# Filling the routed regions with zero rows by bulk copies during the attention, instead of sixteen paddings per region later

## The reference

```python
x = x + tanh(g_xattn[0]) * L0_xattn(layernorm(x), ctx, ctx, ...)
x = x + tanh(g_ffn[0])   * L0_ffn(layernorm(x), ...)
x = x + tanh(g_xattn[1]) * L1_xattn(layernorm(x), ctx, mask, ...)   # 16 heads of 64
x = x + tanh(g_ffn[1])   * L1_ffn(layernorm(x), ...)

def L1_ffn(hidden, ...):            # 4096 tokens, 16 experts, 4 chosen per token
    scores = sigmoid(x @ gate_w.T)
    topk_idx, topk_weight = gate(scores + e_bias)
    inter = silu(x @ gate_proj[e]) * (x @ up_proj[e])
    y = sum_k topk_weight[k] * (inter @ down_proj)[topk_idx[k]]
    return y + shared_expert(x)
```

## Time and profile before

| | us |
|---|---|
| median of three runs | 1568.88 |
| lowest and highest run | 1566.62, 1571.58 |
| the profiled execution, whole | 1582.4 |
| its span, first to last instruction | 1579.9 |
| attention, about | 405 to 1088 |
| second sparse layer, about | 1088 to 1580 |

### The profile page before, as it was taken

How to read it: one execution, slowest core, us unless ns; L and a number is a source line. 1 busy time by engine, 2 the same in 40 slices (tenths; PEclk the granted TensorE clock), 3 DMA queues, 4 the chain that set the end, 5 groups by cost and what they waited for, 6 DMA issues and landing times. The chain is left out here.

```text
span 1579.9 us, 28066 instructions
## 1 busy us (share of the span) xinstructions
PE 1209.1 (77%) x9252; PEld 1095.7 (69%) x9252; DVE 936.1 (59%) x2025; ACT 785.4 (50%) x2201; POOL 530.2 (34%) x658
## 2 busy tenths in 40 slices
PE   3777217998589999999999999975578767668774
PEld 2555116988578888888888888864577756557773
DVE  4887664453366666568666777774556423223666
ACT  3555213554266667666657555554445434335442
POOL 4333243563000001100164005542225555655541
PEclk8566557999799999999999999996779978888987
DMA  3349744553400000000133003333744555545796
GB/s 97 120 135 264 179 102 130 145 147 76 136 7 14 8 1 21 28 8 1 41 119 110 15 1 122 121 101 130 225 144 135 175 165 157 157 125 166 252 289 222
DMA packets 140545, 181.33 MB, mean 115 GB/s; under 512 B 22496, under 2 KB 120960, under 8 KB 139904
## 3 DMA queue, kind: packets, MB, share of 16 engines
q1 hardware_dynamic: 113040, 127.90, 28.2%
q0 software_dynamic: 17792, 43.14, 8.6%
q10 hardware_dynamic: 9584, 8.60, 1.9%
HBM read 111.51 MB, written 72.32 MB: 116 GB/s over the span
## 5 line engine op out<-in xcount | busy, mean ns | idle before, releaser
L1617 ACT ACTIVATE attend_s<-attend_s,attend_less 128x128 f32<-128x128 f32 x512 | 198.4, 391 | 109.1 <-DVE attend_less L1758 102.5
L2283 POOL DMA_INDIRECT answers<-moe_yb,moe_dst x160 | 158.7, 992 | 166.4 <-ACT moe_yb L2373 128.8
L1572 POOL TENSOR_TENSOR router_xn<-rest_acc,router_mv 128x512 f32<-128x512 f32 x12 | 12.5, 1044 | 445.6 <-DVE router_rs L1234 389.5
L81 PE MATMUL moe_psU<-moe_wh,moe_xl 128*128 (+1 forms) x384 | 119.0, 310 | 0.3 <-issue 0.3
L2429 DVE TENSOR_TENSOR moe_it<-moe_it,moe_psU 128x256 f32<-128x256 f32 x96 | 40.2, 419 | 132.9 <-ACT moe_it L2355 98.8
L82 PE MATMUL moe_psU<-moe_wl,moe_xh 128*128 (+1 forms) x384 | 117.7, 307 | 1.1 <-issue 0.8
L83 PE MATMUL moe_psU<-moe_wh,moe_xh 128*128 (+1 forms) x384 | 117.4, 306 | 0.5 <-issue 0.5
L1635 ACT ACTIVATE attend_pt<-attend_psS 128x1024 f32<-128x1024 f32 x64 | 65.5, 1024 | 95.6 <-PE attend_psS L1909 95.5
L1202 POOL DMA_INDIRECT slots<-router_row,router_idx x80 | 82.0, 1025 | 82.0 <-DMA router_row<-normed_rows 63.0
L2582 PE MATMUL moe_psI<-const_ident,moe_it 128*128 128x128 f32 x192 | 42.2, 305 | 85.0 <-DVE moe_il L2425 79.6
L1756 DVE SCALAR_TENSOR_TENSOR attend_s<-attend_psS,held_bias 128x1024 f32<-128x1024 f32 x64 | 77.9, 1217 | 44.2 <-PE attend_psS L1902 44.1
(11 more groups left out here) (376 smaller groups left out, 4238.5 us busy)
## 6 DMA issues: line engine op xcount, KB each, us to landing
moe_xg<-slots SPq DMA_DIRECT2D x160, 129.0 KB
moe_both<-answers SPq DMA_DIRECT2D x28, 512.0 KB
router_row<-normed_rows SPq DMA_DIRECT2D x40, 256.0 KB
layer_raw<-in_wi_dram SPq DMA_DIRECT2D x8, 1024.0 KB, 5.0
layer_raw<-in_wo_dram SPq DMA_DIRECT2D x8, 1024.0 KB, 7.0
moe_raw<-in_gex_dram SPq DMA_DIRECT2D x17, 384.0 KB, 5.0
moe_both<-normed_rows SPq DMA_DIRECT2D x24, 256.0 KB
slots<-fill SPq DMA_DIRECT2D x32, 129.0 KB
```

Source lines behind the costliest of these rows:

```text
L81: pe.matmul(out, wl, mh, start=first, stop=False)
L1617: last = nc.scalar.activation(s[:, g, j, :], s[:, g, j, :], ACT.Exp, bias=less[:, g, j:j + 1], accum_out=sm[:, g, j:j + 1])
L2283: nc.gpsimd.indirect_dma_start(out=R.YT[q], out_offset=bass.IndirectOffsetOnAxis(ap=dst[:, r % NM, s:s + 1], axis=0), in_=yb[:, r % NY, s, ...
```

## The change

Paddings per expert go. In their place SP copies `fill` blocks over the whole of every region, in the attention: at each of steps 0 to 7 two regions of part 0 (25 copies of one block each), at each of steps 8 to 15 two regions of part 1 (9 copies each). The source is one block, read again and again. POOL waits for all of part 0's copies before the first row is sent (half-step 17), and SP waits for all copies at the end of `attend`. The table `tail`, its instruction on VectorE and its waits go. In `moe`, the loads of the rows to be sent are issued one or two pairs earlier, and the last four stores of normalised pairs are issued by ScalarE at j = 1, 3, 5 and 7, instead of by SP.

```diff
+        self.blanked = [m.sem(f"blanked{r}") for r in range(2)]
...
+            def blank(q, e):
+                to = R.XS[q][e * REGION[q]:(e + 1) * REGION[q], :].rearrange("(b p) n -> b (p n)", p=P)
+                tile = R.fill[q][e * P:(e + 1) * P, :].rearrange("p n -> (p n)").unsqueeze(0)
+                sp.dma_start(to, tile.to_broadcast([REGION[q] // P, P * WIDE])).then_inc(R.blanked[q], 16)
...
             def body(n, p, h):
                 if turns(n):
                     load(n + 2, p, h + 1)
+                if n < STEPS // 2:
+                    blank(0, 2 * n)
+                    blank(0, 2 * n + 1)
+                else:
+                    blank(1, 2 * n - E1)
+                    blank(1, 2 * n - E1 + 1)
                 routed(AT[2 * n])
                 routed(AT[2 * n + 1])
...
+            def blanked():
+                sp.wait_ge(R.gw_in, 32)
+                for b in R.blanked:
+                    sp.wait_ge(b, 16 * E1)
...
             normed(1, 0)
+            pool.wait_ge(R.blanked[0], 16 * E1)
             send(0, 0, 1)
...
-            def padded(q, e):
-                if e == 0:
-                    sp.wait_ge(table_up, 2 * q + 1)
-                first = sp.value_load(tail[0:1, q, e:e + 1], min_val=0, max_val=E1 * REGION[q] - P)
-                sp.dma_start(R.XS[q][bass.ds(first, P), :], R.fill[q][e * P:(e + 1) * P, :]).then_inc(pad_in, 16)
...
-                if j in (7, 8):
-                    for h in range(2 * j - 10, 2 * j - 8):
-                        load_row(h)
-                if j in (8, 10, 12, 14):
-                    R.store_normed(sp, LAST, (j - 8) // 2)
-                if 7 <= j < FIRST:
-                    for e in range((j - 7) * 4, min(E1, (j - 6) * 4)):
-                        padded(0, e)
+                for n in range(2):
+                    if 2 * (j - NX) + NR + n < EXPERTS:
+                        weights(2 * (j - NX) + NR + n)
+                    if NS + 2 * (j - NX) + n < FORMER:
+                        load_row(NS + 2 * (j - NX) + n)
...
+                if j - 1 in normed_at:
+                    R.store_normed(act, LAST, normed_at[j - 1])
...
-                v.scalar_tensor_tensor(tail[0:1, q, :], cnt[0:1, :], 1.0, R.ebase[0:1, q, :], ALU.add, ALU.add).then_inc(table_up, 1)
```

More of the change, by code:

```diff
@@ L1552, in body @@
                     load(n + 2, p, h + 1)
+                if n < STEPS // 2:
[4 more added lines that the diff above has]
+                    blank(1, 2 * n - E1 + 1)
                 routed(AT[2 * n])
                 routed(AT[2 * n + 1])
-            over(sp, body, lambda: sp.wait_ge(R.gw_in, 32))
+            def blanked():
+                sp.wait_ge(R.gw_in, 32)
+                for b in R.blanked:
+                    sp.wait_ge(b, 16 * E1)
+            over(sp, body, blanked)
         @block.gpsimd
@@ L2048, in moe @@
         table = sb("table", [1, 2, 2, 64], I32)
-        tail = sb("tail", [1, 2, E1], I32)
         psX, psU, psY = ([ps(f"{n}{k}", [P, 512]) for k in range(2)] for n in ("psX", "psU", "psY"))
@@ L2061, in moe @@
             sem(n) for n in ("w_hi", "w_early", "w_late", "t_done", "x_hi", "x_lo", "u_done", "s_up", "i_up", "i_done", "i_hi", "i_lo", "y_done", "y_up", "d_up", "g_up"))
-        made, r_done, r_free, col_up, table_up, pad_in, marked, c_up, c_step, stored, added = (
-            sem(n) for n in ("made", "r_done", "r_free", "col_up", "table_up", "pad_in", "marked", "c_up", "c_step", "stored", "added"))
+        made, r_done, r_free, col_up, table_up, marked, c_up, c_step, stored, added = (
+            sem(n) for n in ("made", "r_done", "r_free", "col_up", "table_up", "marked", "c_up", "c_step", "stored", "added"))
         block = ctx.enter_context(nc.Block(no_gpsimd_drain=True))
@@ L2181, in ready @@
             def ready(q):
-                sp.wait_ge(table_up, 2 * q + 2)
-                sp.wait_ge(pad_in, 16 * E1 * (q + 1))
+                sp.wait_ge(table_up, q + 1)
                 sent_upto(sp, (FORMER, len(SENDS))[q])
@@ L2224, in _ @@
             for j in range(NX, PAIRS_ALL):
-                for k in (2 * (j - NX) + NR, 2 * (j - NX) + NR + 1):
-                    if k < EXPERTS:
-                        weights(k)
-                if j in (7, 8):
-                    for h in range(2 * j - 10, 2 * j - 8):
-                        load_row(h)
-                if j in (8, 10, 12, 14):
-                    R.store_normed(sp, LAST, (j - 8) // 2)
-                if 7 <= j < FIRST:
-                    for e in range((j - 7) * 4, min(E1, (j - 6) * 4)):
-                        padded(0, e)
+                for n in range(2):
[3 more added lines that the diff above has]
+                        load_row(NS + 2 * (j - NX) + n)
                 if j == STARTS_OF[0]:
@@ L2240, in _ @@
                     load_row(FORMER + i // 2)
-                e = j - placed_at - NX - 4
-                if 0 <= e < E1:
-                    padded(1, e)
                 if j == STARTS_OF[1]:
@@ L2477, in tables @@
                 v.tensor_copy(table[0:1, q], psR[0:1, 0:2 * P].rearrange("p (a j) -> p a j", a=2)[:, :, 0:64]).then_inc(table_up, 1)
-                dve.wait_ge(table_up, 2 * q + 2)
+                dve.wait_ge(table_up, q + 1)
                 dve.sem_inc(r_free, 1)
@@ L2605, in _ @@
                 if j + 1 in STARTS_OF:
-                    pe.wait_ge(table_up, 2 * KIND[j + 1] + 2)
+                    pe.wait_ge(table_up, KIND[j + 1] + 1)
                 if j + 1 < PAIRS_ALL:
```

## The result

The changed kernel takes 1610.94 us (median of 4 runs, 1609.13 to 1615.28), the kernel before, run again beside it, 1567.91 us (4 runs, 1566.62 to 1571.58). The ratio is 1.0275, with a 95% interval of 1.0247 to 1.0302: 43 us slower. The forecast was 1869 us, also slower, but by 300 us. The sign and the places of the stalls came as foretold; the size did not. That 1610.9 lies inside the stated range (1610 to 2090) is luck: it lies 1 us from its foot, and the likeliest case had 1740 to 1955. (The paddings that went are one per region, sixteen per part, and not sixteen per region as the title has it.)

The account below looks back on a forecast made before the run. TensorE was taken to bound the attention, memory and SyncE's order the second sparse layer's first stage. 1582.4 profiled, plus 315 for copies, minus 15 gained, gives 1882; less 13.5, 1869 us, range 1610 to 2090.

Parts of the forecast that it names:

- the likeliest case: Attention's copies on five engines near 16.5 GB/s each (14.7 to 20), 1740 to 1955 us; chance 0.38.
- The equal deal: Attention's copies: the outer count is dealt in equal shares, so 25 blocks go to 5 engines and 9 to 9.
- a rival with sixteen engines: Attention: all engines share each copy, 12.5 us per copy, nothing on TensorE waits, 1554 us; chance 0.19, 0.16 with a gain.
- I take 16.5: Rate of one engine copying memory to memory in the attention, in GB/s; gives 40.0 us per copy of part 0.
- the best end: Attention's copies at the fastest rate taken, 23.9 GB/s per engine: 27.6 us per copy, +101 us, 1655 us.
- The rival of five engines at that rate: Attention's copies on five engines at 23.9 GB/s each: +101, 1655 us; chance of five engines, faster, 0.20.
- The estimate of 13.4 GB/s: Attention's copies: the skill's 214 GB/s shared by 16 engines; would add some 474 us in place of 315.
- The sum: Attention: contexts and stores land late behind copies in SyncE's queue, delaying TensorE's turns by 315 us in all.
- +11: Attention, after the first send: two more meetings of a store with copies in SyncE's queue add 11 us.
- The gain: Second sparse layer's first stage: paddings' issue, their bytes and waits for stores removed, 15 us, bounds 0 and 30.
- The stage of 12 shared pairs: Second sparse layer's first stage: a sign that it would take about 55 us instead of 70.
- Share near 5/16: Attention's steps of 470 to 800 us: a sign of a DMA share about 0.3, with 83 GB/s.

Follow-up runs that it names:

- act_stores: Changed kernel with the attention's twelve stores of pairs issued by ScalarE in its own queue, copies still on five engines from SyncE: 1603.88 us, ratio 1.02 to the kernel before.
- spread16: Changed kernel with the same bytes copied, each copy cut to an outer count of 16 with runs of 8,256 bytes: 1553.79 us, ratio 0.9849 to the kernel before.
- spread4: Changed kernel with each copy cut to an outer count of 4, runs of 33,024 bytes: 1754.87 us, ratio 1.1189 to the kernel before.
- before_copies: Kernel before with the region copies and their two waits added in the attention; its paddings and second sparse layer stay: 1648.7 us, ratio 1.0462 to the kernel before.
- act_queue: Changed kernel with the region copies issued by ScalarE in its own queue, still 25 and 9 blocks: 1645.4 us, ratio 1.0437 to the kernel before.
- act_stores_short: Changed kernel with the attention's stores on ScalarE and each copy made as eight transfers of 16,512-byte runs, still five engines: 1610.18 us, ratio 1.0269 to the kernel before.

## Why the prediction was wrong in size and right in kind

**How many engines: right.** The equal deal was taken against a rival with sixteen engines. The share of 0.33 shows five, outer counts of 16, 8 and 4 give 0.66, 0.52 and 0.28, and of a store's 256 records 80, sixteen for each of five engines, are the late ones (act_stores). The rule of the Trainium skill's page "DMA: Bandwidth & Descriptors", section "Why a DMA increments its semaphore by 16 and not by 1", says the same for 25, and the trace agrees. The rival's time, 1554, is also what the same copies cost when they are cut for sixteen engines, 1553.8; but the kernel before took 1576.6 beside that run, so the rival's gain of 15 us was 24, and the match to the microsecond is luck.

**The rate of an engine: the step that failed.** The prediction said "I take 16.5, as the new transfers have large packets", from queue 8's 1.25 MB in 0.3%, and so 40.0 us per copy. It is 27.06 GB/s and 24.4 us. The rounding of 0.3% was not the fault: in the DMA records of the kernel before, queue 8's packets of 16,384 bytes take 1002 ns in the median, 16.4 GB/s. But that is queue 8, instruction, another kind of transfer, and its size says nothing of a copy. The nearest kin of the copies stood in the same trace: the paddings, also from `fill` to `slots`, are 512 runs of 8,256 bytes, and the fastest takes 309 ns, 26.7 GB/s (474 ns in the median, among the other transfers of a busy stage). The windows had 23.9 GB/s per busy engine. The bounds were too low as well: the best end was 27.6 us per copy. The rival of five engines at that rate (+101, 1655 us) was the right mechanism and came nearest in size, and stood at a chance of 0.20. The estimate of 13.4 GB/s from the Trainium skill's 214 GB/s (same page, section "Latency and other measured facts"), shared by sixteen, is not borne out either: the trace has 27 GB/s for each of five engines, and 280 GB/s for sixteen while spread16's copies ran.

**The sum, done again with 24.4 us.** By the same steps: the context turned at 548.2 lands at 427 + 4 x 24.4 + 3 = 528, not late; that of 625.0 at 625, just in time (5.4 late in the trace). The first store lands at 427 + 244 + 3 = 674, the second pair is turned at 677, 32 late (38); the next store lands at 674 + 48.8 = 723, the third pair is turned at 726, 62 late (70). Steps 6's and 7's copies, issued at 735 and 740, need 98 us and end by 834 (831 in the trace), before POOL needs them at 848, so the "+11" and the wait before the first send fall away. That is 62 us instead of 315, and 1582.4 + 62 - 15 - 13.5 = 1616 for the measured 1610.9. That it comes so near is luck in part, as too little lateness (62 for 68) and too little gain (15 for 24 to 29) cancel. The second and third turn come 6 to 8 us later than in this working; the other transfers among the copies, which the working left at nothing, are of this order (16 us over twelve copies).

**The lateness is no constant times the length.** From 24.4 to 30.5 us per copy it goes from 68 to 184 (spread4), since each turn that comes late lets another store meet other copies. The forecast's copy was 64% too long (40.0 against 24.4 us), and its sum 4.6 times the measured one (315 against 68).

**The gain: 15 us taken, 24 to 29 measured.** spread16 gives 24, before_copies against the changed kernel 29. The profiles give more, 491.7 to 450.8 us for the layer, and before_copies has 492.0 in a run within 3 us of its median; how much of these 41 us is the 13.5 of the one profile, the rows do not decide. The stage of 12 shared pairs was to take 55 us and takes 51.4. The prediction valued the earlier row loads at nothing beyond the 15, and they are worth perhaps 6.

**Only one queue.** The working explains the stalls by SyncE's queue. That is what happens, but it is not needed: with the copies in ScalarE's queue the stalls are as long (act_queue).

**The signs foretold.** Share near 5/16: yes. 83 GB/s: 139. Waits of over 50 us on L1239's turn: two of 31.5 and 29.9, and POOL's of 64.5 behind them. TensorE waiting for context from the third step on: once, 3.9 us. A gap of POOL before the first send: none beyond 6.9 us for a row load. No padding, and a shorter first stage: yes. The clock, for which nothing was added, was 0.57 of 2.4 GHz in the window of 650 to 690, in which TensorE was idle 31 of 40 us, and 0.50 from 710 to 730, its level of 1.2, when it had nothing to do at all; from 740 to 780 it was 1.00 again. It cost little: from the third pair's turn to the fourth's it took 22.9 us instead of 21.3.

So the 43 us are some 68 lost in the attention, by copies that use five engines, and 24 to 29 won in the second layer. The two sizes agree with the difference and with the experiments that have one without the other. The version that keeps the gain and not the loss is the one with an outer count of 16 or 8: 1553.8 and 1543.4 us, 0.985 and 0.984 of the kernel before, which their intervals do not tell apart. That is 4% below the changed kernel.

## What to carry to other kernels

Cut a large copy so that its outer count is 16, or 8, and read the DMA share of a step afterwards: a share that stands at 5/16 while the copy runs says that eleven engines are idle. Before large transfers are put into an idle stretch, add up their time on the engines that they will really use, and compare it with the stretch up to the first thing that waits for them all; another queue does not help against full engines, and there a small transfer pays one run of the copy for each of its own records on such an engine. For the price of a transfer that no row shows, look for its nearest kin in the trace, by source and destination and not by size alone, take the fastest run of it, and work the sum at both ends, as a chain of stores and waits magnifies the error.

## What the runs showed of the hardware

- From memory to memory one engine moved 26.8 to 27.1 GB/s with four, five or eight engines at work (runs of 16.5 to 44 KB in 615 to 1627 ns, median). With sixteen a run of 8,256 bytes took 312 ns in the median and 384 in the mean of the window of 450 to 490, 21.5 GB/s. While two copies ran, all sixteen moved 280 GB/s (800 runs in 23.6 us), eight 214; the windows' 224 and 216 are near each other only because the sixteen were done early and idle for the rest.
- Beside engines full of another queue's copies, a transfer of 256 records of 1,024 bytes had 176 of them, those of the eleven free engines, started within 4 us, and the other 80 came one per full engine after each run of the copies (act_stores, act_stores_short). The last ended 25 to 29 us after the issue beside runs of 44,032 bytes and 12.6 to 12.8 beside runs of 16,512.
- SyncE's issue stands still when much is outstanding. In the changed kernel two issues of a copy took 1.5 us at 512.5, with between two and three earlier copies unfinished, but 24.8 us at 550.6, with about three, and 24.5 us at 626.6, with two, a store and a context load. Sixteen issues of the shorter ones took 47 to 52 us. What exactly fills up, no run shows.
- TensorE was not slowed by 224 GB/s of transfers: 38.45 of 40 us busy, 38.43 without them.
